# Second layer of a two-layer transformer kernel: fifteen contexts projected before the first batch, and x3 laid into the PSUM bank by ScalarE

## The chip, the cores and the metric

One Trainium2 chip, one of its cores. The kernel is one program for the core's five engines: TensorE (PE in the profile, its weight loads PEld), VectorE (DVE), ScalarE (ACT), GpSimd (POOL) and SyncE (SP, which here issues most DMAs). The metric is device time in microseconds, the median of several executions. One further execution is profiled; its rows give start and duration of each instruction.

## The reference

The input is 16 batches of 256 rows by 256 columns, with a context of 120 rows per batch. There are two layers. The first is attention and a mixture of experts; it fills the first 820 us and the change does not touch it. The second layer, cut to what matters:

```python
x = x + attention(layernorm(x), ctx, ctx, mask, Wq, Wk, Wv)   # gives x4 from x3
x = x + linear(quantise(layernorm(x)), quantise(weight)) + bias
# attention: K = ctx Wk, V = ctx Wv, softmax(Q K^T / 16, masked) V, one head of 256
# quantise: blocks of 32, scale = max|x| / 7.5, nearest point of the FP6 grid, times the scale
```

Everything is float32 on TensorE. The kernel multiplies Wk and Wq together beforehand, so that a batch's scores need only the normalised rows and one projected context ("keys"), and the values are a second projection of the same context.

## The kernel before

`second_phase` is written as one program per engine. A batch goes through some twenty steps on four engines, and the batches are overlapped by hand: a loop over a cycle number c runs on each engine (`CYCLES`, from -4 to 19), and in one cycle the engine does step A of batch c, step B of batch c-1, step C of batch c-3 and so on. Each engine works through its list strictly in order and waits on semaphores, so the order of the calls in each loop sets what can hide behind what.

The names that matter, with n the batch:

- Contexts. `turn_context(n)` (PE transposes, L2313), `keep_context` (ACT, L2181), `keys(n)` (PE, L2336), `keep_keys` (ACT, L2185), `values(n)` (PE, L2344), `keep_values` (ACT, L2189). The first `EARLY` = 9 contexts are projected in a loop ahead of the cycles, while the rows of the first batches are still being fetched and normalised. The other seven are projected inside cycles -1 to 5, one in each.
- Rows. `stats_acc`, `centre`, `residual` (DVE) build x3 from the experts' sum and the residual x2; `stats_x3` (DVE), `inverse_std(N3)` (POOL), `normalise_x3` (ACT, L2154), `turn_rows` (PE, L2325), `keep_xnT` (ACT, L2175).
- Attention. `scores` (PE, L2357) into the bank `zp_ps`, `bounded` (DVE, L2098 and L2102), `exps` (ACT, L2199), `inverse_sums` (DVE, L2125), `diagonals` (ACT, L2211), `turn_probs` (PE, L2367), `keep_probsT` (ACT, L2220), `weigh` (PE, L2377). `weigh` adds to a PSUM bank `f_ps` (a ring of three, one per batch) that already holds x3: `start_result` (PE, L2287) put it there with a matmul of the identity. So after `weigh` the bank holds x4.
- Second norm, quantisation and the last matmul. `stats_x4` (DVE, L2040, reading f_ps), `inverse_std(N4)` (POOL, L1993 to L2002), `normalise_x4` (ACT, L2154, reading f_ps), `scales` (DVE), `to_blocks` (POOL, L2011), `round_blocks` (ACT, L2228), `scale_back` (POOL, L2020), `turn_quantised` (PE, L2278), `keep_xdT` (ACT, L2236), `linear` (PE, L2298 for the bias and L2303), `keep_result` (ACT, L2243), and the store by SP.

The expert phase's last matmul ends on PE before the contexts begin; the rows of the experts' sum are loaded only when the last scattered additions of the expert phase have landed (`past["added"]` in SP's list).

Of the kernel before, what the change touches and what calls it, by code (L numbers as in the profile page):

```python
# [56 lines left out]
RING = 3  # L57
# [1736 lines left out]
def second_phase(nc, sem, past, ident, second, mask, x2_d, acc_d, ctx, out):  # L1794
# [7 lines left out]
    with st:  # L1802
# [101 lines left out]
        s_dg = sem("c_diagonal_ready")  # L1904
        s_xn4 = sem("c_xn4_ready")
# [28 lines left out]
        EARLY = 9  # L1934
# [4 lines left out]
        def sync(sp):  # L1939
# [35 lines left out]
            for c in range(-5, B + 4):  # L1975
                if exists(c - 2):
                    sp.wait_ge(s_o, c - 1)
                    sp.dma_start(rows(out, c - 2), o[c % 2][:]).then_inc(s_ost[c % 2], 16)
                if RING <= c + 5 < B:
                    load_x2(c + 5)  # L1980
                if RING <= c + 8 < B:
                    load_acc(c + 8)
# [3 lines left out]
        def gpsimd(pool):  # L1986
# [40 lines left out]
            for c in CYCLES:  # L2027
                inverse_std(NA, c + 3, s_x3)
                inverse_std(N3, c + 2, s_xn3)
                to_blocks(c - 1)  # L2030
                inverse_std(N4, c, s_xn4)
                scale_back(c - 1)

        def vector(dve):
# [104 lines left out]
            for c in CYCLES:  # L2139
                bounded(c)  # L2140
                residual(c + 2)
                inverse_sums(c)
                stats_x3(c + 2)
                centre(c + 3)
                scales(c - 1)
                stats_acc(c + 4)
                stats_x4(c)

        def scalar(act):
# [64 lines left out]

            def keep_probsT(n):
                if not exists(n):
                    return
                act.wait_ge(s_pT_p, n + 1)
                ge(act, s_o_p, n - 1)
                act.copy(pT[n % 2][0:CTX], pT_ps).then_inc(s_pT, 1)  # L2220
# [30 lines left out]
            for c in CYCLES:  # L2251
                exps(c - 1)
                normalise_x4(c - 2)
                diagonals(c - 1)
                if late(c + 9):
                    keep_keys(c + 9)
                keep_result(c - 4)
                keep_probsT(c - 1)
                if late(c + 9):
                    keep_values(c + 9)  # L2260
                keep_xdT(c - 3)
                keep_xnT(c)
                if EARLY < c + 10 < B:
                    keep_context(c + 10)
                normalise_x3(c + 1)
                round_blocks(c - 2)

        def tensor(pe):
# [12 lines left out]

            def start_result(n):
                if not exists(n):
                    return
                pe.wait_ge(s_x3, n + 1)
                ge(pe, s_o, n - 2)
                pe.matmul(f_ps[n % RING][:].rearrange("p u d -> p (u d)"), ident[:],  # L2287
                          x3[n % RING][:].rearrange("p u d -> p (u d)"),
                          start=True, stop=False, skip_group_check=True)
# [81 lines left out]
            def weigh(n):  # L2371
# [3 lines left out]
                pe.wait_ge(s_v, n + 1)  # L2375
                for u in range(2):
                    j = pe.matmul(f_ps[n % RING][:, u, :], pT[n % 2][0:CTX, u, :], vv[n][0:CTX, :],  # L2377
                                  start=False, stop=True, skip_group_check=True)
# [7 lines left out]
            for s, value in past["experts"]:  # L2386
                pe.wait_ge(s, value)
            for c in CYCLES:
                turn_quantised(c - 3)
                turn_probs(c - 1)  # L2390
                start_result(c - 1)
                weigh(c - 1)
                if EARLY < c + 10 < B:
                    turn_context(c + 10)
# [3 lines left out]
                if late(c + 10):  # L2398
                    keys(c + 10)
                if late(c + 10):  # L2400
                    values(c + 10)
# [25 lines left out]
```

## Time and profile before

| | us |
|---|---|
| median of 3 runs | 972.43 |
| lowest, highest | 972.27, 979.09 |
| the profiled execution | 978.93 |
| span of its instructions | 977.2 |
| last expert matmul group ends on PE, first context turned | 819.55 |
| context 1 turned (starts) | 820.46 |
| last early `values` starts (ninth context) | 837.31 |
| first `scores` (batch 0) | 843.31 |
| `scores`, eight matmuls: after a wait, and in a stream | 1.12, 1.05 |
| `linear`, eight matmuls in the steady cycle | 1.99 |
| `weigh` of batches 0, 2, 15 | 848.60, 862.46, 959.27 |

Times inside the profile are counted from the start of the span. PE is busy 97% of the span, yet in a pipelined kernel this is an average: whether PE or a chain of waits sets the pace has to be read stage by stage. A start of one instruction less the start of the next on the same engine is the distance that counts for a queue, since consecutive instructions overlap a little; an instruction that waits for another one's result starts only after the recorded end of that other one.

### The profile page before, as it was taken

How to read it: one execution, taken by the hardware profiler on the slowest of the kernel's cores; microseconds unless marked ns; L12 is line 12 of the kernel's file. 1: busy time of each engine (PE TensorE's matmuls, PEld its weight loads, DVE VectorE, ACT ScalarE, POOL GpSimd, SP SyncE). 2: the span in 40 equal slices, each digit the busy share in tenths (PEclk: the TensorE clock that was granted, in tenths of full speed). 3: DMA queues.
4: the chain of work that ended last, by engine and by line, in shares of the span. 5: the costliest groups of instructions: out<-in, count | busy, mean ns of one | idle time of the engine just before them, and what ended most of it. 6: DMA issues, size and time to landing. Idle time of an engine off the chain costs nothing.

```text
span 977.2 us, 22166 instructions
## 1 busy us (share of the span) xinstructions
PE 944.5 (97%) x7195; PEld 804.6 (82%) x7195; DVE 515.9 (53%) x1268; ACT 519.7 (53%) x1326; POOL 495.2 (51%) x660
## 2 busy tenths in 40 slices
PE   6999999999989999998999999999999999899997
PEld 4777777677758999998999999999999998777774
DVE  3788898888874543533223223232232232787862
ACT  3777877777754743333333333333333333678884
POOL 2444344565763148765554444445344442576773
PEclk9999999999999999999999999999999999999999
DMA  5234454355433455333342221222222217423311
GB/s 171 88 121 151 139 173 133 101 151 160 147 115 99 143 161 70 33 34 47 48 65 39 42 40 29 39 34 35 43 33 39 39 32 188 122 86 93 115 53 46
DMA packets 86126, 85.38 MB, mean 87 GB/s; under 512 B 19296, under 2 KB 81184, under 8 KB 85888
## 3 DMA queue, kind: packets, MB, share of 16 engines
q1 hardware_dynamic: 70336, 65.28, 21.9%
q0 software_dynamic: 15680, 18.69, 13.1%
q8 instruction: 62, 1.02, 0.5%
q14 instruction: 48, 0.39, 0.2%
HBM read 52.54 MB, written 31.39 MB: 86 GB/s over the span
## 4 chain that ended last, share of the span: by engine, by line
PE 88%; DVE 3%; issue 2%; ACT 2%; POOL 2%; another core or an unknown queue 1%; SPq 1%; DMA 1%; DVEq 0%; POOLq 0%; ACTq 0%
PE b_H L1582 25%; PE b_Y L1603 24%; PE a_T L939 5%; PE a_O L953 4%; PE c_f_ps L2303 3%; PE a_S L919 3%; PE a_M L988 3%; PE a_O L894 2%; PE c_f_ps L2298 2%; PE b_xT L1571 2%; PE a_T L905 2%; PE c_f_ps L2287 1%; PE c_zp_ps L2357 1%; PE c_f_ps L2377 1%
## 5 line engine op out<-in xcount | busy, mean ns | idle before, releaser
L1752 ACT ACTIVATE b_hiddenT<-b_H,b_b 128x128 f32<-128x128 f32 x568 | 162.3, 369 | 320.5 <-PE b_H L1582 276.9
L1582 PEld LDWEIGHTS b_H<-b_rowsT,b_w 128*128 128x128 f32 x2272 | 264.7, 192 | 7.4 <-ACT b_rowsT L1759 3.0
L1582 PE MATMUL b_H<-b_rowsT,b_w 128*128 128x128 f32 x2272 | 265.6, 275 | 2.8 <-ACT b_rowsT L1759 2.6
L1603 PE MATMUL b_Y<-w_sb,b_hiddenT 128*128 x1136 | 257.5, 379 | 1.1 <-issue 1.0
L1521 POOL DMA_INDIRECT ffn_rows<-b_y,b_slots x71 | 138.7, 1953 | 197.3 <-DVE b_y L1687 115.3
L1603 PEld LDWEIGHTS b_Y<-w_sb,b_hiddenT 128*128 128x128 f32 x1136 | 210.4, 190 | 27.7 <-issue 2.0
L1683 DVE TENSOR_TENSOR b_y<-b_Y,b_b 128x256 f32<-128x256 f32 x71 | 30.2, 425 | 300.2 <-PE b_Y L1603 279.2
L1510 POOL DMA_INDIRECT b_rows<-xn_rows,b_slots x71 | 75.3, 1060 | 68.0 <-PE b_xT L1571 49.7
L1670 DVE COPY b_w<-w_sb 128x2048 f32 x71 | 87.8, 1237 | 35.3 <-issue 29.8
L1243 ACT COPY a_probsT<-a_T 120x512 f32<-120x512 f32 x128 | 74.8, 586 | 46.2 <-PE a_T L939 37.3
L423 POOL DMA_INDIRECT buckets<-r_pay,r_place x64 | 70.6, 1103 | 24.4 <-issue 19.4
L1076 DVE TENSOR_REDUCE a_max<-a_S 128x8 f32<-128x960 f32 x64 | 73.6, 1150 | 13.4 <-PE a_S L919 13.1
L939 PE MATMUL a_T<-ident,a_probs 128*120 128x128 f32 x512 | 77.0, 278 | 3.3 <-ACT a_probs L1235 3.1
L1084 DVE TENSOR_TENSOR a_probs<-a_S,a_max 128x960 f32<-128x960 f32 x64 | 73.2, 1144 | 0.7
L939 PEld LDWEIGHTS a_T<-ident,a_probs 128*120 128x120 f32 x512 | 56.8, 138 | 15.7 <-issue 9.3
L1235 ACT ACTIVATE a_probs<-a_probs 128x960 f32<-128x960 f32 x64 | 64.5, 1008 | 9.0 <-DVE a_probs L1084 6.8
L953 PE MATMUL a_O<-a_probsT,a_vaug 120*32 120x128 f32 x1024 | 54.3, 285 | 0.4 <-ACT a_probsT L1243 0.3
L953 PEld LDWEIGHTS a_O<-a_probsT,a_vaug 120*32 120x32 f32 x1024 | 20.2, 108 | 28.9 <-issue 23.1
L785 POOL TENSOR_TENSOR a_x<-a_x,a_xin 128x256 f32<-128x256 f32 x16 | 12.4, 774 | 48.2 <-DVE a_x L1097 43.0
L988 PE MATMUL a_M<-a_wsg,a_xn2T 128*128 128x264 f32 x128 | 35.6, 401 | 0.2 <-ACT a_xn2T L1258 0.2
L919 PE MATMUL a_S<-a_kbd,a_qT 32*128 32x240 f32 x512 | 35.0, 387 | 0.9 <-ACT a_qT L1219 0.8
L2303 PEld LDWEIGHTS c_f_ps<-c_wdT,c_xdT 128*128 128x128 f32 x128 | 23.4, 193 | 14.8 <-issue 12.1
(237 smaller groups left out, 1322.5 us busy)
## 6 DMA issues: line engine op xcount, KB each, us to landing
w_sb<-in_L_ffn_W SPq DMA_DIRECT2D x32, 512.0 KB
x_rows<-a_x SPq DMA_DIRECT2D x32, 128.0 KB
xn_rows<-a_xn SPq DMA_DIRECT2D x32, 128.0 KB
shared_rows<-a_shared SPq DMA_DIRECT2D x32, 128.0 KB
b_spare<-shared_rows SPq DMA_DIRECT2D x16, 256.0 KB
ffn_rows<-b_spare SPq DMA_DIRECT2D x16, 256.0 KB
c_x<-x_rows SPq DMA_DIRECT2D x16, 256.0 KB, 3.0
c_acc<-ffn_rows SPq DMA_DIRECT2D x16, 256.0 KB, 2.7
```

Of the source, the lines that this page charges most:

```text
L423: pool.indirect_dma_start(bucket_d, IndirectOffsetOnAxis(place[:, t, k:k + 1], 0), pay[:, t, k, :], None).then_inc(s_put[g // 2], 16)
L939: i = pe.transpose(T_ps[q % 2][0:CTX, j * P:(j + 1) * P], pr[q // 2][:, 4 * (q % 2) + j, :], ident[:])
L953: i = pe.matmul(O_ps[VB * j:VB * (j + 1), q * P:(q + 1) * P], vaug[t // 2 % 2][0:CTX, 4 * q + j, :], pT[q % 2][0:CTX, j, :], start=True, s ...
L1076: dve.tensor_reduce(mx[h][:].rearrange("p (r j) -> p r j", r=RG), scores_of(h), AX.X, ALU.max).then_inc(s_mx, 1)
L1084: dve.tensor_tensor(pr[h][:].rearrange("p (r j) c -> p r j c", r=RG), scores_of(h), mx[h][:].rearrange("p (r j) -> p r j", r=RG).unsqueeze ...
L1243: act.copy(pT[q % 2][0:CTX].rearrange("p j n -> p (j n)"), T_ps[q % 2][0:CTX, :]).then_inc(s_T, 1)
L1510: pool.indirect_dma_start(xg[n % AHEAD][:], None, xn2_d, IndirectOffsetOnAxis(iw[:].bitcast(I32)[:, n, 0:1], 0)).then_inc(s_x[n % AHEAD], 16)
L1521: pool.indirect_dma_start(acc_d, IndirectOffsetOnAxis(iw[:].bitcast(I32)[:, n, 0:1], 0), y[n % KEPT_Y][:], None, bounds_check=TOK + SPARE - 1,
L1582: j = pe.matmul(H_ps[i][:, c * P:(c + 1) * P], w1c[i][:, k * HID + c * P:k * HID + (c + 1) * P], xT[:, k * P:(k + 1) * P], start=(k == 0), ...
L1603: j = pe.matmul(y_ps[i][:, 0:D], hT[i][:, c * P:(c + 1) * P], w2_sb[:, bass.ds(e * (HB * D) + c * D, D)], start=(c == 0), stop=(c == HB - 1))
L1670: dve.tensor_copy(w1c[i][:], w1_sb[:, bass.ds(e * (KC * HID), KC * HID)])
L1752: j = act.activation(hT[i][:, c * P:(c + 1) * P], H_ps[i][:, c * P:(c + 1) * P], ACT.Gelu, bias=b1c[i][:, c:c + 1])
```

## The change

Three things are done, and the loops are put in another order.

1. `EARLY` is 15: fifteen contexts are projected ahead of the cycles, and only the sixteenth inside cycles -1 and 0. The loads, turns and keeps move with them; none is added or dropped.
2. `start_result` on PE is gone. A new step `lay_x3(n)` on ACT copies x3 into the bank f_ps, between `keep_result` and `keep_probsT`. It waits for the semaphore of `keep_result`, the instruction just ahead of it in ACT's own queue. `weigh` waits for it. So that a matmul that adds finds the bank in the state it needs, each of the three banks gets one matmul of 128x512 ahead of the cycles (discarded values).
3. Orders. On PE, `turn_probs` and `turn_quantised` trade places and move to the end of a cycle's list (with their batch numbers one up, so in time only the two are exchanged). On DVE the list is only rotated: the sequence in time is the same. On POOL, `scale_back` moves from ahead of the next `inverse_std(NA)` to behind it. On ACT, `keep_xnT` and `keep_context` go ahead of `keep_xdT`. SP issues the loads of x2 one cycle earlier and those of the experts' sum one cycle later, relative to the stores.

```diff
--- before.py
+++ after.py
@@ -1902,6 +1902,8 @@
         s_o_p = sem("c_x4_psum")
         s_rs = sem("c_rs_ready")
         s_dg = sem("c_diagonal_ready")
+        s_laid = sem("c_x3_laid")
+        s_banks = sem("c_banks_written")
         s_xn4 = sem("c_xn4_ready")
         s_am = sem("c_amax_ready")
         s_sc = sem("c_scale_ready")
@@ -1931,7 +1933,7 @@
 
 
 
-        EARLY = 9
+        EARLY = 15
 
         def late(n):
             return EARLY <= n < B
@@ -1972,14 +1974,14 @@
                 load_acc(n)
             for n in range(CTX_RING + 2, B):
                 load_context(n)
-            for c in range(-5, B + 4):
+            for c in range(-4, B + 4):
                 if exists(c - 2):
                     sp.wait_ge(s_o, c - 1)
                     sp.dma_start(rows(out, c - 2), o[c % 2][:]).then_inc(s_ost[c % 2], 16)
-                if RING <= c + 5 < B:
-                    load_x2(c + 5)
-                if RING <= c + 8 < B:
-                    load_acc(c + 8)
+                if RING <= c + 6 < B:
+                    load_x2(c + 6)
+                if RING <= c + 7 < B:
+                    load_acc(c + 7)
             for i in range(2):
                 sp.wait_ge(s_ost[i], 8 * B)
 
@@ -2026,10 +2028,10 @@
             pool.memset(ones[:], 1.0).then_inc(s_tie, 1)
             for c in CYCLES:
                 inverse_std(NA, c + 3, s_x3)
+                scale_back(c - 2)
                 inverse_std(N3, c + 2, s_xn3)
                 to_blocks(c - 1)
                 inverse_std(N4, c, s_xn4)
-                scale_back(c - 1)
 
         def vector(dve):
             def stats(g, src, n):
@@ -2137,14 +2139,14 @@
                 bounds(part)
             dve.wait_ge(second["s_vec"], 32)
             for c in CYCLES:
+                residual(c + 1)
+                inverse_sums(c - 1)
+                stats_x3(c + 1)
+                centre(c + 2)
+                scales(c - 2)
+                stats_acc(c + 3)
+                stats_x4(c - 1)
                 bounded(c)
-                residual(c + 2)
-                inverse_sums(c)
-                stats_x3(c + 2)
-                centre(c + 3)
-                scales(c - 1)
-                stats_acc(c + 4)
-                stats_x4(c)
 
         def scalar(act):
             def normalise(g, dst, src, n, done):
@@ -2211,6 +2213,15 @@
                     j = act.activation(dg[n % 2][:, u, :], ident[:], ACT.Identity,
                                        scale=rs[n % 2][:, u:u + 1])
                 j.then_inc(s_dg, 1)
+
+            def lay_x3(n):
+                if not exists(n):
+                    return
+                act.wait_ge(s_x3, n + 1)
+                if n == 0:
+                    act.wait_ge(s_banks, RING)
+                ge(act, s_o, n - RING + 1)
+                act.copy(f_ps[n % RING][:], x3[n % RING][:]).then_inc(s_laid, 1)
 
             def keep_probsT(n):
                 if not exists(n):
@@ -2252,16 +2263,17 @@
                 exps(c - 1)
                 normalise_x4(c - 2)
                 diagonals(c - 1)
-                if late(c + 9):
-                    keep_keys(c + 9)
+                if late(c + 15):
+                    keep_keys(c + 15)
                 keep_result(c - 4)
+                lay_x3(c - 1)
                 keep_probsT(c - 1)
-                if late(c + 9):
-                    keep_values(c + 9)
+                if late(c + 15):
+                    keep_values(c + 15)
+                keep_xnT(c)
+                if EARLY < c + 16 < B:
+                    keep_context(c + 16)
                 keep_xdT(c - 3)
-                keep_xnT(c)
-                if EARLY < c + 10 < B:
-                    keep_context(c + 10)
                 normalise_x3(c + 1)
                 round_blocks(c - 2)
 
@@ -2278,15 +2290,6 @@
                         j = pe.transpose(xdT_ps[:, u, k, :],
                                          xd[n % 2][:, u, k * P:(k + 1) * P], ident[:])
                 j.then_inc(s_xdT_p, 1)
-
-            def start_result(n):
-                if not exists(n):
-                    return
-                pe.wait_ge(s_x3, n + 1)
-                ge(pe, s_o, n - 2)
-                pe.matmul(f_ps[n % RING][:].rearrange("p u d -> p (u d)"), ident[:],
-                          x3[n % RING][:].rearrange("p u d -> p (u d)"),
-                          start=True, stop=False, skip_group_check=True)
 
             def linear(n):
                 if not exists(n):
@@ -2373,6 +2376,7 @@
                     return
                 pe.wait_ge(s_pT, n + 1)
                 pe.wait_ge(s_v, n + 1)
+                pe.wait_ge(s_laid, n + 1)
                 for u in range(2):
                     j = pe.matmul(f_ps[n % RING][:, u, :], pT[n % 2][0:CTX, u, :], vv[n][0:CTX, :],
                                   start=False, stop=True, skip_group_check=True)
@@ -2385,20 +2389,24 @@
                 values(n)
             for s, value in past["experts"]:
                 pe.wait_ge(s, value)
+
+            for bank in f_ps:
+                pe.matmul(bank[:].rearrange("p u d -> p (u d)"), ident[:],
+                          wdT[:].rearrange("p k d -> p (k d)"), start=True, stop=True,
+                          skip_group_check=True).then_inc(s_banks, 1)
             for c in CYCLES:
-                turn_quantised(c - 3)
-                turn_probs(c - 1)
-                start_result(c - 1)
                 weigh(c - 1)
-                if EARLY < c + 10 < B:
-                    turn_context(c + 10)
+                if EARLY < c + 16 < B:
+                    turn_context(c + 16)
                 scores(c)
                 linear(c - 3)
                 turn_rows(c + 1)
-                if late(c + 10):
-                    keys(c + 10)
-                if late(c + 10):
-                    values(c + 10)
+                if late(c + 16):
+                    keys(c + 16)
+                if late(c + 16):
+                    values(c + 16)
+                turn_probs(c)
+                turn_quantised(c - 2)
 
         return Programs(sync, gpsimd, tensor, vector, scalar)
 
```

## Rows read from the trace of the kernel before

**Rows 1.** The page: busy time of each engine over the whole span.

```profile
PE 944.5 (97%) x7195; PEld 804.6 (82%) x7195; DVE 515.9 (53%) x1268; ACT 519.7 (53%) x1326; POOL 495.2 (51%) x660
```

**Rows 2.** Busy time by stretch, mostly weigh to weigh: stretch, length, busy by engine, granted clock.

```profile
838.35:843.31 4.96, 2.59 (x19) 2.25 (x19) 3.03 (x11) 2.73 (x8) 3.30 (x8) 1.00 0.45 132
848.60:855.53 6.93, 5.93 (x38) 4.63 (x36) 5.94 (x22) 5.18 (x16) 4.33 (x12) 1.00 0.25 77
871.39:880.31 8.92, 8.92 (x52) 6.96 (x50) 6.41 (x23) 6.80 (x19) 5.87 (x12) 1.00 0.30 89
910.37:917.36 6.99, 6.99 (x38) 5.25 (x37) 6.30 (x24) 5.90 (x17) 5.63 (x13) 1.00 0.39 115
968.00:977.20 9.20, 5.24 (x18) 3.15 (x16) 0.00 (x0) 1.76 (x3) 0.47 (x1) 0.85 0.16 57
```

**Rows 3.** Timeline of PE: first and last early values, then the first batch.

```profile
821.59 1.03 PE L2344 MATMUL c_v_ps<-c_wv,c_ctxT 128*120 128x256 f32 x4
...
837.31 1.03 PE L2344 MATMUL c_v_ps<-c_wv,c_ctxT 128*120 128x256 f32 x4
839.89 0.63 PE L2325 MATMUL c_xnT_ps<-ident,c_xn 128*128 128x128 f32 x4 [1.54 <-ACT c_xn L2154]
...
843.31 1.12 PE L2357 MATMUL c_zp_ps<-c_gT,c_xnT 128*128 128x120 f32 x8 [0.83 <-ACT c_xnT L2175]
```

**Rows 4.** SP's queue: the last six context loads are issued.

```profile
830.13 2.88 SPq L1946 DMA_DIRECT2D c_ctx<-in_ctx  x6
```

**Rows 5.** The chain that ended last, one steady cycle: start, length, what.

```profile
908.71 0.44 PE c_xdT_ps L2278 x4
909.15 0.44 PE c_zp_ps L2367 x4
909.59 0.95 PE c_f_ps L2287 x2
```

**Rows 6.** Timeline of DVE in a steady cycle.

```profile
911.44 0.76 DVE L2040 BATCH_NORM_STATS2 c_x_bn<-c_f_ps 128x6 f32<-128x256 f32 x2 [0.33 <-PE c_f_ps L2377]
912.40 0.38 DVE L2098 SCALAR_TENSOR_TENSOR c_z<-c_zp_ps,c_bound 128x240 f32<-128x240 f32 x1
```

**Rows 7.** Timeline of POOL, the same cycle.

```profile
913.91 0.20 POOL L2002 TENSOR_TENSOR c_x_nb<-c_x_nm,c_x_rstd 128x2 f32<-128x2 f32 x1
914.06 1.05 POOL L2020 TENSOR_TENSOR c_xd<-c_q,c_amax 128x512 f32<-128x512 fp8e4 x1
915.08 0.23 POOL L1993 TENSOR_SCALAR c_acc_ve<-c_acc_mv 128x2 f32<-128x2 f32 x1
...
916.29 0.22 POOL L1993 TENSOR_SCALAR c_x_ve<-c_x_mv 128x2 f32<-128x2 f32 x1
```

**Rows 8.** Timeline of ACT, the same cycle.

```profile
913.25 0.40 ACT L2199 ACTIVATE c_probs<-c_z,c_nmax 128x120 f32<-128x120 f32 x1 [0.68 <-DVE c_nmax L2102]
...
914.21 1.02 ACT L2154 ACTIVATE c_xn<-c_f_ps,c_x_nb,c_x_rstd 128x256 f32<-128x256 f32 x2
915.12 0.69 ACT L2211 ACTIVATE c_diagonal<-ident,c_rs 128x128 f32<-128x128 f32 x2
915.71 0.57 ACT L2243 COPY c_out<-c_f_ps 128x512 f32<-128x512 f32 x1
```

**Rows 9.** Timeline of ACT in batch 0, and PE's weight load behind it.

```profile
846.45 0.70 ACT L2211 ACTIVATE c_diagonal<-ident,c_rs 128x128 f32<-128x128 f32 x2 [0.23 <-DVE c_rs L2125]
...
847.94 0.37 ACT L2220 COPY c_probsT<-c_zp_ps 120x256 f32<-120x256 f32 x1 [0.55 <-PE c_zp_ps L2367]
...
852.48 1.02 ACT L2154 ACTIVATE c_xn<-c_f_ps,c_x_nb,c_x_rstd 128x256 f32<-128x256 f32 x2
...
848.36 0.43 PEld L2377 LDWEIGHTS c_f_ps<-c_v,c_probsT 120*128 120x128 f32 x2 [0.43 <-ACT c_probsT L2220]
```

**Rows 10.** Groups of ACT by shape, whole span: busy, mean ns of one.

```profile
L1461 ACT ACTIVATE b_spare<-b_spare 128x512 f32<-128x512 f32 x16 | 9.6, 651 | 0.0
L2243 ACT COPY c_out<-c_f_ps 128x512 f32<-128x512 f32 x16 | 9.3, 580 | 5.2 <-PE c_f_ps L2303 5.2
```

**Rows 11.** Timeline of PE: the linear layer of batch 14, in the drain.

```profile
966.44 2.90 PE L2303 MATMUL c_f_ps<-c_wdT,c_xdT 128*128 128x256 f32 x8
```

## The prediction

> **What bounds the kernel now.** The page [rows 1] shows PE busy 97% of the span. That invites the reading that taking work off PE is worth its length, so the second layer has to be read in parts. The windows [rows 2] are cut from one `weigh` (W below) to the next. Three regimes are seen. From 848.60 to 855.53 PE is busy 5.93 of 6.93 us: although a context is projected in that cycle, PE waits for others. From 871.39 to 880.31 it is busy all 8.92 us, again with a context. From 910.37 to 917.36, with no context, it is busy all 6.99 us, while DVE has 6.30 and ACT 5.90. So contexts cost nothing in the first two cycles and about 1.93 us in each of the next three (W2 to W5, with numbers for batches).
>
> How near is the next limit in the steady cycle? Follow one batch's x4 through the timelines. W starts at 910.37; DVE's `stats_x4` starts at 911.44 [rows 6]; POOL ends the N4 factors at 913.91 + 0.20 = 914.11 [rows 7]; ACT's `normalise_x4` starts at 914.21 [rows 8]. That is 3.84 us. ACT's next instruction is `diagonals` for the batch behind (0.91 later, 915.12), and `turn_probs` and `weigh` of that batch need it. This closes a loop with a length of one cycle: W, stats_x4, N4, normalise_x4, diagonals, turn_probs, W. Before the change it closes over PE: diagonals to turn_probs is 0.70 of duration and 0.04 to start, then 0.44 and 0.95 for turn_probs and start_result [rows 5, 9]: 3.84 + 0.91 + 0.74 + 0.44 + 0.95 = 6.88. PE's own list takes 6.99. Only 0.11 us separate PE, which looks like the bound, from this chain. That distance is what the case turns on.
>
> **The change, part by part.**
>
> *Six more contexts in front.* The early loop repeats every (837.31 - 821.59) / 8 = 1.965 us [rows 3]. Six more: +11.79. ACT's `normalise_x3` of batch 0 stands behind all `keep_values` in ACT's list, so it moves too; nothing of the first batch gets on PE earlier. Their loads were all issued by 830.13 + 2.88 = 833.01 [rows 4]. The first of them (context 10) is turned at about 820.46 + 9 x 1.965 = 838.2, 5 us later: no stall.
>
> *Three bank matmuls.* Each is a 128x512 matmul like start_result, 0.86 in its shorter form (0.95 in rows 5): 2.6 us. Before `turn_rows` of batch 0, PE now waits 1.54 [rows 3], which hides that much. Left: +1.04. With 0.95 each it would be +1.3.
>
> *First batches.* `scores` of batch 0 follows 3.42 after its turn_rows [rows 3], as before, since one context (now the sixteenth) still stands between. Scores to diagonals takes 3.14 (843.31 to 846.45). From diagonals to `keep_probsT` is 1.49 [rows 9], set by turn_probs; `lay_x3` fits in front of it (0.59 + about 0.52 = 1.11). From keep_probsT to W I take 0.50: 0.37 of duration and 0.13, between the weight load's 0.42 (848.36 - 847.94) and 0.60. So scores to W is 5.13 instead of 5.29 (-0.16). The next two periods were 6.93 each. Now they are W to normalise_x4 3.88 (848.60 to 852.48) + 0.91 + 1.49 + 0.50 = 6.78: -0.15 each, -0.30.
>
> *Steady cycle, W2 to W15, 13 periods.* From batch 3 on `keep_result` stands in ACT's list as well. The loop now runs diagonals, keep_result, lay_x3, keep_probsT, all in one queue. W to normalise_x4 3.84, to diagonals 0.91, to keep_result 0.59 [rows 8]. lay_x3 waits for keep_result's own semaphore: it starts after its recorded end, 0.57 + 0.04 = 0.61, instead of overlapping it by 0.10 as ACT's instructions otherwise do (914.21 + 1.02 against 915.12), which would be 0.47. Lay_x3 itself: no row has ACT writing PSUM. The nearest ones [rows 10] are a PSUM to SBUF copy of this shape, 0.580, and an SBUF to SBUF activate, 0.651; less about 0.10 of overlap that gives 0.48 to 0.55; I take 0.52. keep_probsT to W 0.50. W now starts on an idle PE, for which I add 0.06 (the eight matmuls of `scores` took 1.12 after a wait and 1.05 in a stream). Sum: 3.84 + 0.91 + 0.59 + 0.61 + 0.52 + 0.50 + 0.06 = 7.03 us. PE's list is down to 6.99 - 0.95 = 6.04 and no longer matters. Thirteen periods took 959.27 - 862.46 = 96.81 and now take 91.4: -5.4. All of that comes from the context cycles that got shorter, and none from start_result.
>
> The Trainium skill ("ScalarE: Activation LUTs", section "Step-by-step: what each stage is for") says that an ACTIVATE into PSUM is faster than one into SBUF. By that the lower end, 0.48, would hold, 0.5 us less in all. The same page's "Rules for kernel authors" gives about 0.3 us and 0.83 ns per element, an estimate of 0.72 for 512 elements, some 1.8 us more in all. Neither is used in the sum.
>
> *Orders.* Moving `scale_back` behind inverse_std(NA) puts it 916.29 - 915.08 = 1.21 us later [rows 7], ending (15.27 + 1.05 against 14.21) about 2.10 after normalise_x4 starts; turn_quantised, 0.60 or so, then runs until 2.75, ahead of W at 3.13. The cover is 0.38; without it the excess would come on each period. The rotated DVE list changes nothing in time. keep_xnT ahead of keep_xdT follows PE's need. SP's loads land well over a cycle ahead in both forms. The last `weigh` to the end of the span (17.93 us, 959.27 to 977.2) keeps its sequence: 0.
>
> *Sum.* +11.79 + 1.04 - 0.16 - 0.30 - 5.4 = +7.0 us on a span of 977.2. The profiled execution took 978.93, 6.5 above the median of 972.43; the runs themselves lie between 972.27 and 979.09. The change is local, so I put the same difference on the median: 979.4 us.
>
> **Rivals.**
>
> - *The ACT stretch hides, DVE sets the pace.* If keep_result and lay_x3 cost 0.76 instead of 1.13, DVE's own list is next: 6.99 less its idle 0.33 [rows 6] = 6.66. Then 13 x 6.66 = 86.6, and the total is +2.2: 974.6. For it: the terms are small. Against it: the wait on keep_result is in the code. A result below the old time needs a period under about 6.5, under DVE's list; 2 in 100.
> - *Slower, by the same loop at its upper ends.* The price is the period: the self-wait at 0.75 instead of 0.61, lay_x3 at 0.61, keep_probsT to W 0.60, W on an idle PE 0.07 more. That is 7.03 + 0.14 + 0.09 + 0.10 + 0.01 = 7.37 and 13 x 0.34 = +4.4: 983.8. It decides against the kernel by over 1% from a period of 7.24 on.
> - *TensorE's clock.* PE will idle about 1.0 us per cycle in two pieces. In the drain the clock is 0.85 [rows 2], and `linear` of batch 14 took 2.90 [rows 11] where it takes 1.99 at the full level (of 1.2 and 2.4 GHz). If that came in each cycle, turn_probs would be reached 0.57 late and more; a period of about 7.5, 13 x 0.47 = +6.1: 985.5. Against it: from 838.35 on PE is busy 2.59 of 4.96, then 5.93 of 6.93, and the clock stays 1.00 [rows 2]. The Trainium skill ("TensorE: Matmul & The Clock Gate", section "What's actually happening") has the rule behind it: the default is throttled and activity releases it, so idle that a change adds to PE can cost more than its length.
> - *PE is the bound as the page says* and the period falls to 6.04: 13 x 6.04 = 78.5, a total of -5.9, 966.5. The 0.11 us of slack and DVE's list speak against it; it is the kernel's hoped-for case, and I count it in the 2 in 100 above.
>
> **How the numbers follow.** Forecast (period 6.85 to 7.2) 0.65, DVE sets the pace 0.14, upper ends 0.12, clock 0.05, below the old time 0.02, something unseen 0.02. The likeliest gives 979.4. For the range: below, the DVE case at 974.6 is nearly taken in; above, the upper ends at 983.8, and room for a median that falls at the upper of the times shown: 975.0 to 985.5. About 1% (9.7 us) is what a measurement of this kernel can tell from no change: the bounds are 962.7 and 982.2. Faster 0.02. Slower: upper ends, clock, and a median from the upper of the times shown (0.06), 0.23. The same: 0.75.
>
> **What would show it.** Early `values` would run fifteen times, to about 849; the first scores would start near 856.1, W0 near 861.2, W2 near 874.8, W15 near 966. In the steady cycle PE would idle about 1.0 us before turn_probs and before W, with ACT named as the releaser, lay_x3 would start 0.04 after keep_result ends, and the period would be 7.03 with the clock at 1.00. The prediction is wrong if the period is 6.7 or less, if PE is still busy without a gap, or if W to normalise_x4 is no longer 3.8.

## The result

The changed kernel takes 985.7 us (median of 4, 983.68 to 989.32) where the kernel before takes 972.35 (median of 4, 971.3 to 979.09). The ratio is 1.014, with a 95% interval of 1.011 to 1.017: slower by 13.4 us. I had forecast 979.4 and a range up to 985.5. The direction is right (the chance I gave to "slower by over 1%" was 0.23), the size is half of what came, and the result lies just outside the range.

The page of the profile answers to [rows 1]: PE is busy a little less, and the kernel is longer.

```profile
PE 942.2 (95%) x7169; PEld 805.3 (82%) x7169; DVE 522.6 (53%) x1268; ACT 530.3 (54%) x1342; POOL 497.8 (50%) x660
```

The span is 987.6 us. What lies ahead of the second layer is the same program in both kernels (817.17 us here, 819.55 before, and between 811 and 821 in the runs below), so the profiles are compared from the first context turned to the end of the span. Each column is cut from the timeline of PE by the same instructions (us):

| part | before | forecast | changed kernel |
|---|---|---|---|
| first context turned to first `turn_rows` | 20.34 | 33.2 | 33.01 |
| to `weigh` of batch 0 (W0) | 8.71 | 8.55 | 8.95 |
| W0 to W2 | 13.86 | 13.56 | 16.61 |
| W2 to W15 | 96.81 | 91.4 | 94.84 |
| W15 to the end | 17.93 | 17.9 | 17.02 |
| sum | 157.65 | 164.6 | 170.43 |

The sum grows by 12.78, in line with the medians' 13.35. The forecast's 7.0 is short by 5.8: 3.05 in the first two periods, 3.4 in the thirteen after them, 0.4 ahead of W0; the drain gave 0.9 back and the front 0.2.

The windows from weigh to weigh answer to [rows 2] (stretch, length, busy time of PE, PEld, DVE, ACT, POOL, granted clock):

```profile
859.13:867.38 8.25, 5.32 (x21) 4.35 (x21) 5.41 (x19) 4.73 (x14) 3.99 (x11) 0.69 0.19 64
867.38:875.74 8.36, 5.66 (x24) 5.12 (x25) 6.80 (x25) 5.59 (x15) 6.16 (x13) 0.72 0.24 65
875.74:883.66 7.92, 7.54 (x35) 5.58 (x34) 6.78 (x22) 6.31 (x17) 5.47 (x12) 0.86 0.12 38
927.54:934.85 7.31, 6.57 (x35) 4.87 (x35) 6.95 (x24) 6.48 (x17) 5.72 (x13) 1.00 0.34 108
949.46:956.50 7.04, 6.56 (x34) 4.86 (x34) 5.37 (x21) 6.49 (x17) 5.50 (x13) 1.00 0.10 38
```

Two things stand out. In the first three periods TensorE's clock is down, and they are the ones that I had wrong most (by 1.5, 1.6 and 0.9 us). And there are two steady periods, 7.31 from batch 3 to batch 12 and 7.04 behind it: the second is my 7.03.

PE in the first batches (its timeline; the bracket is the idle time before and what ended it):

```profile
857.46 1.21 PE L2370 MATMUL c_zp_ps<-c_diagonal,c_probs 128*120 128x128 f32 x4 [2.33 <-ACT c_diagonal L2213]
859.13 2.07 PE L2381 MATMUL c_f_ps<-c_v,c_probsT 120*128 120x256 f32 x4 [0.46 <-ACT c_probsT L2231]
861.00 1.90 PE L2360 MATMUL c_zp_ps<-c_gT,c_xnT 128*128 128x120 f32 x8
```

`weigh` takes 2.07 us and `scores` 1.90, where they took 1.03 and 1.05 in the steady cycle: the lower of the two levels, 1.2 GHz. Before them PE stands idle for 2.33 us, where a context used to be projected. The lower level comes and goes: by turn_probs of batch 1 the clock was back (0.70 us, at 866.22), and `weigh` behind it was slow again (1.79).

In the steady cycle the timelines of DVE and POOL answer to [rows 6, 7]:

```profile
925.40 1.60 DVE L2055 SCALAR_TENSOR_TENSOR c_centred<-c_acc,c_acc_mv,c_gamma 128x256 f32<-128x256 f32 x2
...
929.01 0.73 DVE L2042 BATCH_NORM_STATS2 c_x_bn<-c_f_ps 128x6 f32<-128x256 f32 x2
```

```profile
924.60 0.71 POOL L2000 TENSOR_TENSOR c_acc_rstd<-c_acc_ve,c_minus_half 128x2 f32<-128x2 f32 x1
925.28 1.05 POOL L2022 TENSOR_TENSOR c_xd<-c_q,c_amax 128x512 f32<-128x512 fp8e4 x1
```

The pair of `centre` takes 1.60 us; before it took 0.85 in every cycle. It starts 0.12 us after `scale_back`, which runs to 926.33. The instructions of this line over the whole span, before and now (shortest, median, longest in ns):

```profile
L2053 DVE SCALAR_TENSOR_TENSOR c_centred<-c_acc,c_acc_mv,c_gamma x32: 450/476/486, 832.6 to 936.5; 128x256 f32<-128x256 f32 x32
L2055 DVE SCALAR_TENSOR_TENSOR c_centred<-c_acc,c_acc_mv,c_gamma x32: 450/476/1207, 830.1 to 948.5; 128x256 f32<-128x256 f32 x32
```

`stats_x4` at 929.01 has no idle time in front of it: DVE has become the bound, and W (927.54) to stats_x4 is 1.47 instead of 1.07.

ACT's timeline answers to [rows 8]:

```profile
924.43 1.02 ACT L2156 ACTIVATE c_xn<-c_f_ps,c_x_nb,c_x_rstd 128x256 f32<-128x256 f32 x2
925.34 0.68 ACT L2213 ACTIVATE c_diagonal<-ident,c_rs 128x128 f32<-128x128 f32 x2
925.93 0.58 ACT L2254 COPY c_out<-c_f_ps 128x512 f32<-128x512 f32 x1
926.59 0.59 ACT L2224 COPY c_f_ps<-c_x 128x512 f32<-128x512 f32 x1
927.12 0.37 ACT L2231 COPY c_probsT<-c_zp_ps 120x256 f32<-120x256 f32 x1
```

keep_result to lay_x3 is 0.66 (forecast 0.61), lay_x3 to keep_probsT 0.53 (0.52), keep_probsT to weigh 0.42 (0.50 and 0.06 for the idle PE), diagonals to keep_result 0.59.

### The profile page after: what moved, and what is told of

Read it like the earlier page. It is cut to its first block, busy times and chain, and to the rows that moved or that the text cites. A ratio compares the mean times of both kernels' runs of the same rounds, so it can differ in the third digit from the quotient of the medians.

```text
span 987.6 us, 22137 instructions
## 1 busy us (share of the span) xinstructions
PE 942.2 (95%) x7169; PEld 805.3 (82%) x7169; DVE 522.6 (53%) x1268; ACT 530.3 (54%) x1342; POOL 497.8 (50%) x660
## 4 chain that ended last, share of the span: by engine, by line
PE 82%; DVE 9%; ACT 3%; issue 3%; POOL 2%; DMA 2%; POOLq 0%; SPq 0%; DVEq 0%; ACTq 0%
PE b_H L1582 26%; PE b_Y L1603 25%; PE a_T L939 5%; PE a_O L953 4%; PE a_M L988 3%; PE a_O L894 3%; PE a_S L919 3%; PE a_T L905 2%; DVE c_x_bn L2042 2%; PE b_xT L1571 2%; PE c_v_ps L2347 1%; DVE c_centred L2055 1%; PE c_xdT_ps L2339 1%; PE a_O L880 1%; PE a_M L965 1%
## 5 line engine op out<-in xcount | busy, mean ns | idle before, releaser
L423 POOL DMA_INDIRECT buckets<-r_pay,r_place x64 | 71.0, 1110 | 24.1 <-issue 18.4
```

The costliest lines, as they stand in the source:

```text
L423: pool.indirect_dma_start(bucket_d, IndirectOffsetOnAxis(place[:, t, k:k + 1], 0), pay[:, t, k, :], None).then_inc(s_put[g // 2], 16)
```

## The experiments

Two causes are to be tested, each against a rival: the clock in the first batches (theory 2) and the collision of `centre` with `scale_back` (theory 1). The times of the runs scatter by several us from chip to chip and run to run, so beside the ratio each run is read by the parts of its one profiled execution, which repeat to some hundredths where the clock is at 1.00. Each ratio is to the kernel before, run beside it on the same chip.

### GpSimd's order put back

```diff
             for c in CYCLES:
+                scale_back(c - 2)
                 inverse_std(NA, c + 3, s_x3)
-                scale_back(c - 2)
                 inverse_std(N3, c + 2, s_xn3)
```

> The changed kernel with scale_back put back ahead of inverse_std(NA) on GpSimd. Theory 1 (VectorE's centre is held up while GpSimd's scale_back runs): every pair of centre takes about 0.85 us again instead of 1.60, the period from weigh to weigh of batches 3 to 12 falls from 7.31 us to the 7.04 us that the changed kernel has once no centre is left, and the time falls by about 9 x 0.27 = 2.4 us. Rival (ScalarE's queue with the added copy sets 7.31): the period stays at 7.31 and the time does not move. The first two periods (8.25 and 8.36 us) stay in either case.

Measured: every period from batch 4 on is 7.03 or 7.04, and centre is back:

```profile
926.68 0.85 DVE L2055 SCALAR_TENSOR_TENSOR c_centred<-c_acc,c_acc_mv,c_gamma 128x256 f32<-128x256 f32 x2
```

W3 to W15 falls from 86.92 to 84.81 us, 2.1 (expected 2.4). The ratio to the kernel before is 1.0126 (1.0101 to 1.0151), which can't be told from that of the change (1.011 to 1.017): the gain is seen in the periods, not in the medians. The profile's first three periods were 8.16, 8.96 and 8.38 with the clock down, so part of the gain was lost there. The sum is 168.81. Theory 1 holds; ScalarE's queue does not make 7.31.

### GpSimd's order alone, in the kernel before

```diff
             for c in CYCLES:
                 inverse_std(NA, c + 3, s_x3)
+                scale_back(c - 2)
                 inverse_std(N3, c + 2, s_xn3)
                 to_blocks(c - 1)
                 inverse_std(N4, c, s_xn4)
-                scale_back(c - 1)
```

> The kernel before with only scale_back moved behind the next inverse_std(NA) on GpSimd, as the change does. Theory 1: centre takes 1.60 us in the steady cycle, VectorE's list becomes 6.66 + 0.75 and the period of batches 5 to 12 rises from 6.99 to about 7.3 to 7.4 us: +2.3 to +3 us. Rival (the order on GpSimd is free, since it is busy 5.6 of 7 us): no change.

Measured: a ratio of 1.0062 (1.0042 to 1.0083) and a sum of 162.96, +5.3. The steady period is 7.57 to 7.58, more than either account gave.

```profile
918.33 1.60 DVE L2053 SCALAR_TENSOR_TENSOR c_centred<-c_acc,c_acc_mv,c_gamma 128x256 f32<-128x256 f32 x2
```

```profile
919.32 0.65 PE L2278 MATMUL c_xdT_ps<-ident,c_xd 128*128 128x128 f32 x4 [0.46 <-POOL c_xd L2020]
```

The collision comes as expected, but it is not what sets 7.57. `stats_x4` starts 1.07 us after W (913.53 and 914.60), as before, 0.15 us behind the instruction ahead of it, so VectorE is not yet the bound. What sets the period is that PE waits 0.46 us for the late result of scale_back, since in this kernel turn_quantised stands ahead of turn_probs; the changed kernel exchanges these two, and there turn_quantised has no wait in front of it. So this run shows that the order alone makes centre 1.60 us long; the price of the collision in the changed kernel is that of the first experiment, and the +5.3 here is not it (0.4 of it is the drain).

### Work for TensorE in the first batches

```diff
                 turn_rows(c + 1)
+                if c in range(0, 3):
+                    pe.wait_ge(s_v, B)
+                    for _ in range(3 - (c == 0)):
+                        pe.matmul(v_bank[:], ident[:], wdT[:].rearrange("p k d -> p (k d)"),
+                                  start=True, stop=True, skip_group_check=True)
```

> The changed kernel with 2, 3 and 3 unused matmuls of 128x512 into the free bank of the values in cycles 0, 1 and 2 (8 matmuls, about 6.9 us of TensorE work that it would otherwise idle). Theory 2 (the first batches are slow because TensorE, idle without the contexts, falls to 1.2 GHz): the granted clock stays at 1.00, weigh of batch 0 to weigh of batch 2 takes 13.6 instead of 16.6 us, batch 2 to 3 about 7.3 instead of 7.9, and the time falls by about 3.5 us although work was added. Rival (the first batches are slow by their chain over VectorE, GpSimd and ScalarE alone): no change, or slower by what the added matmuls delay.

Measured: the mean clock over the span is 1.000, W0 to W2 takes 13.26 (two periods of 6.63) instead of 16.61, W2 to W3 7.67 instead of 7.92 (7.3 expected; it is 7.03 once GpSimd's order is put back as well, below), and the sum is 166.29: 4.1 us less with 8 matmuls more. The ratio of the times is 1.0121 (1.0089 to 1.0153); its interval overlaps that of the change, so the gain is shown by the parts and not by the medians. The two windows that hold W0 to W2:

```profile
859.90:866.50 6.60, 5.92 (x27) 3.65 (x27) 5.80 (x22) 4.85 (x14) 4.24 (x12) 1.00 0.25 82
866.50:873.10 6.60, 6.15 (x30) 4.03 (x30) 6.31 (x22) 5.46 (x15) 5.08 (x12) 1.00 0.24 79
```

Work that nobody needs makes the stretch 3.35 us shorter. By the rival, a chain over the other engines alone, it would have stayed. With the clock up that chain is the 6.63 (forecast 6.78).

### Fifteen early contexts alone, in the kernel before

```diff
-        EARLY = 9
+        EARLY = 15
```

(with the loops' offsets 9 and 10 made 15 and 16)

> The kernel before with 15 early contexts instead of 9 and nothing else. My account (a context in front costs 1.965 us each, one in a cycle costs 1.93 only in cycles 3 to 5 and nothing in 0 to 2): +11.8 in front, -5.9 in the three cycles of 8.92 us, so +5.9 us; if the clock falls in the first batches, some 3 us more, +9. Rival (contexts cost the same wherever they stand, since TensorE is busy 97%): 0.

Measured: a ratio of 1.0074 (1.0044 to 1.0104), a sum of 166.54, +8.9 us. Front +11.8, W0 to W2 +2.8 with the clock down, W2 to W15 -6.1 (90.70), drain +0.4. A context in front costs its length; in the first cycles it costs nothing and keeps the clock up; only the three later cycles give TensorE's time for it back. W0 to W1 took 9.60 and W1 to W2 7.09; a window that holds most of W0 to W1:

```profile
860.00:870.00 10.00, 7.11 (x24) 5.27 (x23) 7.39 (x28) 5.50 (x16) 5.90 (x14) 0.70 0.26 79
```

### Both causes mended

> The changed kernel with both edits of the first two runs: scale_back ahead of inverse_std(NA), and 2, 3 and 3 unused matmuls in cycles 0 to 2. If the two causes are the whole error of my forecast and are independent, the clock stays at 1.00, weigh of batch 0 to 2 takes 13.3 us, the thirteen periods after it 7.04 each (91.5 us), and from the first context turned to the end of the span it takes 33.0 + 8.4 + 13.3 + 91.5 + 17.0 = 163.2 us against 157.65 before: slower by 5.6 us, near the +7.0 that I had forecast. If something else is at work it is 165 or more.

(The edit is that of the first and the third experiment together.) Measured: 33.01 + 8.44 + 13.25 + 91.37 = 146.07 up to W15, where 146.2 was expected. All thirteen periods are 7.02 or 7.03. The drain took 18.41 instead of 17.0, so the sum is 164.48. The ratio is 1.0065 (1.0041 to 1.0089), 6.4 us on 978 (the medians, 983.08 and 978.12, differ by 5.0). On another chip the first edit alone had 1.0126 and the filler alone 1.0121, with intervals that begin at 1.0101 and 1.0089, so the two together show in the times as well. Up to W15 the changed kernel takes 153.41, with the filler 149.29, with both 146.07, and my forecast was 146.7: taken in this order the clock is worth 4.1 us and GpSimd's order 3.2. The two causes are thus the error of the forecast up to W15, and the sum with both mended is +6.8, where I had worked out +7.0.

### Half of the copy

```diff
-                act.copy(f_ps[n % RING][:], x3[n % RING][:]).then_inc(s_laid, 1)
+                act.copy(f_ps[n % RING][:, 0, :], x3[n % RING][:, 0, :]).then_inc(s_laid, 1)
```

> The first of those edits alone (GpSimd order put back), and lay_x3 copies only the first of the two halves of x3, 256 instead of 512 columns (left out: the second half, so the second half of the rows is not right). Theory (the steady period of 7.04 us is the loop weigh, stats_x4, N4, normalise_x4, diagonals, keep_result, lay_x3, keep_probsT, which has no slack): the copy is shorter by about 0.2 us and the period falls by the same, to about 6.84. Rival (VectorE's or TensorE's list sets 7.04): it stays at 7.04.

(On top of GpSimd's order put back; one execution.) Measured: 6.82 or 6.83 in each steady period, where the first experiment had 7.04. The copy is 0.38 instead of 0.59 us, and the next instruction follows 0.31 after it instead of 0.52.

```profile
932.08 0.38 ACT L2224 COPY c_f_ps<-c_x 128x256 f32<-128x256 f32 x1
932.39 0.37 ACT L2231 COPY c_probsT<-c_zp_ps 120x256 f32<-120x256 f32 x1
```

A copy shorter by 0.21 us shortens every steady period by 0.21 to 0.22. With the collision away, the loop through ScalarE sets the steady cycle, without slack.

### Nine early contexts, the rest of the change kept

```diff
-        EARLY = 15
+        EARLY = 9
```

> The changed kernel with nine early contexts, as before: the copy on ScalarE, the bank matmuls and the orders alone. My account: front 20.3 + 1.0 us for the bank matmuls, no loss of clock in the first batches (a context stands in each cycle), TensorE's 7.97 instead of 8.92 us in the three cycles with context and full list (3 x -0.95), then 7.31 instead of 6.99 while centre collides with scale_back (about 7 x +0.32) and 7.04 after (3 x +0.05): about +0.5 us from the first context to the end, against +12.8 for the whole change. Rival (the copy on ScalarE is what makes the change slow): +5 us or more.

Measured: a ratio of 1.0028 (1.0000 to 1.0057) and a sum of 159.05, +1.4 us. W0 to W2 is 13.59, steady 7.30 and then 7.03, as expected; but the three context cycles took 8.62, 8.55 and 8.56, not 7.97. My account left out what start_result had covered: without it PE waits between turn_quantised and weigh for keep_probsT (0.17 us). The timeline of ACT says more: in such a cycle keep_keys waits 0.62 us for `keys`, and keep_result, lay_x3 and keep_probsT follow it in the same queue, 1.88 us from keep_keys (888.24) to W (890.12). That this queue sets 8.55 is read from the timeline and not tested by itself. Of the 12.8 us of the change, all but 1.4 come with the six contexts in front.

### Nine early contexts, order put back, short bank matmuls

```diff
+            half_ident = ident[:].bitcast(BF16)
             for bank in f_ps:
-                pe.matmul(bank[:].rearrange("p u d -> p (u d)"), ident[:],
-                          wdT[:].rearrange("p k d -> p (k d)"), start=True, stop=True,
-                          skip_group_check=True).then_inc(s_banks, 1)
+                for u in range(2):
+                    j = pe.matmul(bank[:, u, :], half_ident[:, 0:P], half_ident,
+                                  start=(u == 0), stop=(u == 1), skip_group_check=True)
+                j.then_inc(s_banks, 1)
```

> Nine early contexts, the copy on ScalarE, GpSimd's order put back, and the three bank matmuls made in bfloat16 (two of 128x256 each, some 0.3 us a bank instead of 0.9), so that they fit into the 1.54 us that TensorE waits there anyway. Account: front 20.3, first batches 8.5 + 13.6, batches 2 to 15 three periods of 7.97 and ten of 7.04 = 94.3, tail 17 to 18: about 154.3 us against 157.65 before, 3 us faster than the kernel before. Rival (the copy is of no use anywhere): no faster than before.

Measured: front 20.25, so the bank matmuls are hidden; steady 7.03; context cycles 8.55 again; sum 156.74, 0.9 less than before. The ratio is 1.0015 (0.9988 to 1.0042): no difference that can be told. The 3 us that I expected did not come: 1.7 of them lie in batches 2 to 15, most of that in the context cycles, and the rest in the drain (18.39).

### turn_probs ahead of the context

```diff
+                if c >= 3:
+                    turn_probs(c)
                 if late(c + 10):
                     keys(c + 10)
                 if late(c + 10):
                     values(c + 10)
-                turn_probs(c)
+                if c < 3:
+                    turn_probs(c)
```

(on top of the previous kernel, with keep_keys behind keep_probsT on ScalarE from cycle 4 on)

> The previous kernel (nine early contexts, copy on ScalarE, GpSimd's old order, short bank matmuls) with turn_probs ahead of keys and values on TensorE from cycle 3 on, and keep_keys behind keep_probsT on ScalarE from cycle 4 on. In the three cycles with a context and a full list TensorE idled 0.34 us behind turn_probs, since start_result no longer covers keep_probsT, and the wait was seen as a period of 8.55. With the context matmuls between turn_probs and weigh the period should be TensorE's own list, 8.0: 3 x -0.5 = -1.5 us, 155.2 from the first context to the end (before: 157.65). Rival (the 8.55 is TensorE's own work): no change.

Measured: a miss. The context cycles took 8.85, 8.75 and 8.75, the ratio is 1.0001 (0.9974 to 1.0029).

```profile
873.12 0.70 PE L2372 MATMUL c_zp_ps<-c_diagonal,c_probs 128*120 128x128 f32 x4 [0.38 <-ACT c_diagonal L2213]
```

turn_probs now comes before its diagonals are ready, and the context matmuls stand between it and weigh: the loop got longer by the very work that had lain beside it.

### A fourth bank, the copy out of the loop

```diff
+        FOUR = 7
+        f_ps = [f_ring[n % RING] if n < FOUR else (v_full, f_ring[1], f_ring[2], f_ring[0])[(n - FOUR) % 4]
+                for n in range(B)]
...
-                lay_x3(c - 1)
+                if c - 1 < FOUR:
+                    lay_x3(c - 1)
...
                 round_blocks(c - 2)
+                if c >= FOUR:
+                    lay_x3(c)
```

(The diff is cut to its main lines. It stands on top of the previous kernel; e11 is the same with turn_probs and keep_keys back where the changed kernel has them.)

> As e9, and from batch 7 on the bank of the values, free by then, is a fourth bank in the ring, so that lay_x3 no longer needs keep_result just before it and stands at the end of ScalarE's cycle, outside the loop. The loop is then weigh to normalise_x4 3.84, diagonals 0.91, 1.49 over turn_probs to keep_probsT, 0.43 to weigh = 6.67, beside VectorE's list of 6.6: a period of 6.65 to 6.75 instead of 7.03 for the eight periods from batch 7 on, -2.5 us, about 152.5 from the first context to the end, 5 us less than before. Rival (keep_result and lay_x3 are not what sets 7.03): no change against e9.

> As e10 with the fourth bank, but with turn_probs and keep_keys where they stand in the changed kernel (e9's edit made the three context cycles 8.75 to 8.85 instead of 8.55 to 8.62, since turn_probs then waits 0.38 us for the diagonals and the context matmuls stand between it and weigh). Account: 20.3 + 8.5 + 13.6 + 3 cycles of 8.57 + 7.0 + 9 of 6.74 + 17 to 18 = 152.6 from the first context to the end, against 157.65 before and 153.2 in e10: 0.5 us faster than e10, about 0.5 per cent faster than the kernel before. Rival (the gain of e10 was the spread of the runs): a ratio of 1.00.

Measured: with the fourth bank the steady period is 6.73 to 6.75 from batch 6 on in both. The first of the two (with the misplaced turn_probs) has a ratio of 0.9961 (0.9926 to 0.9996) and a sum of 153.17. The second has 0.9931 (0.9908 to 0.9954), 968.11 against 974.41 us in the same group of runs: it beats the kernel before by 0.7% (0.5% expected), and the changed kernel, which took 985.16 us in that group, by 17 us. Its profiled execution has a sum of 157.71 all the same, since in it the clock was at the lower level through the drain, which took 21.95 instead of 17.0. Up to W15 it took 135.76, against 139.72 before. The window in the drain:

```profile
957.00:969.20 12.20, 8.26 (x18) 4.64 (x17) 0.00 (x0) 1.75 (x3) 0.00 (x0) 0.50 0.12 43
```

The copy now stands behind round_blocks, and the queue between diagonals and keep_probsT waits for turn_probs instead (ACT's timeline, e10):

```profile
939.64 0.58 ACT L2230 COPY c_f_ps<-c_x 128x512 f32<-128x512 f32 x1
...
942.63 0.57 ACT L2260 COPY c_out<-c_f_ps 128x512 f32<-128x512 f32 x1
943.51 0.37 ACT L2237 COPY c_probsT<-c_zp_ps 120x256 f32<-120x256 f32 x1 [0.31 <-PE c_zp_ps L2381]
```

### The change once more

> The changed kernel itself once more, beside the others on one chip. The parts should repeat: 33.0 from the first context turned to the first turn_rows, 9.0 to weigh of batch 0, 16.6 to 17 to batch 2 with the clock below 0.9, 7.31 in the steady cycles with centre, 7.04 after; a ratio of 1.011 to 1.017 to the kernel before.

Measured: 33.01, 8.82, 17.65 (more than the 16.6 to 17 expected: 8.76 and 8.89, with the clock at 0.50 and 0.69 in them), 7.30 and 7.03; a ratio of 1.0114 (1.0085 to 1.0143). The lower clock in the first batches stands in every profile with fifteen early contexts and no filler, its length not quite the same.

## Why the prediction was right in sign and short in size

*What bounds the kernel.* Right. PE at 97% was not the bound to go by: the loop over stats_x4, N4, normalise_x4 and ScalarE's queue was 0.11 us behind it by my sum, and taking 0.95 us off PE bought nothing in the steady cycle. The steady period without the collision is 7.04, 7.03 forecast, and halving the copy moved it one for one.

*Six contexts and the bank matmuls in front.* Right: 12.67 measured, 12.83 forecast.

*First batches.* This is the step that failed most: -0.30 forecast, +2.75 measured. The chain was worked out well (6.63 with the clock up, 6.78 forecast), but at the lower clock weigh and scores take nearly twice as long (2.07 and 1.90 us), and they then make a longer way round: the softmax of the next batch stands ahead of normalise_x4 in ACT's list, and it waited for those scores.

```profile
863.81 0.40 ACT L2201 ACTIVATE c_probs<-c_z,c_nmax 128x120 f32<-128x120 f32 x1 [3.21 <-DVE c_nmax L2104]
```

W to normalise_x4 took 5.45 in this period (3.88 forecast, 3.82 in the filled run), which is more than the whole of the 1.47 by which the period was off. The clock was among my rivals, at 0.05, and I looked for it in the steady cycle. There it stayed at 1.00 with PE busy 6.57 of 7.31. What I held against it was that the clock stays up in the first batches of the kernel before, with PE busy 2.59 of 4.96 and then 5.93 of 6.93 [rows 2]. Those 5.93 contain the context that the change takes out: I had used a row of before for a stretch whose content the change removes. Less the 1.96 of the context and the start_result, PE's share is near 3.1 of 6.8, and no row of before shows that from one weigh to the next. The row of 2.59 of 4.96 is as thin, but it is one stretch alone, and the one behind it was full in the kernel before. From the first scores to W0, before and in the changed kernel:

```profile
843.31:848.60 5.29, 4.92 (x31) 3.79 (x32) 3.91 (x13) 3.57 (x13) 0.99 (x3) 1.00 0.05 15
853.58:859.13 5.55, 2.76 (x16) 2.22 (x17) 4.15 (x14) 3.30 (x11) 1.26 (x3) 0.85 0.14 47
```

The Trainium skill ("TensorE: Matmul & The Clock Gate", section "What's actually happening") says that activity is what keeps the throttle off; here the filled run (5.92 of 6.60, clock 1.00) and the change (5.32 of 8.25, 0.69, much of it at half speed) agree with it. The 0.4 us ahead of W0 have the same cause: that part is 8.95 where turn_probs of batch 0 took 1.21, and 8.44 in the runs with the filler, where it took 0.70.

*Orders.* The second failure. I priced the later scale_back by its reader alone (0.38 us of cover, which held in the changed kernel) and put its effect on DVE at nothing. (That the rotated list of DVE is free was right: with it and GpSimd's old order the period is 7.04.) In the kernel before, scale_back ran from 914.06 to 915.11 [rows 7], and centre began just clear of it (the timeline of DVE of the kernel before):

```profile
915.18 0.85 DVE L2053 SCALAR_TENSOR_TENSOR c_centred<-c_acc,c_acc_mv,c_gamma 128x256 f32<-128x256 f32 x2
```

Moved by 1.21 us in my sum and by 1.00 as measured against the start of normalise_x4, it lies on centre. The pair grows by 0.75, the 0.33 us of idle that DVE had is gone, and DVE's list, 7.31, is the period. (6.66 and 0.75 would be 7.41; stats_x4 also starts 0.08 us closer to the instruction ahead of it once it need not wait.) W to normalise_x4 becomes 4.21 (920.22 to 924.43), which my own list of signs has as one of being wrong. Nine periods at 0.28 over the forecast are 2.5 us, and W2 to W3, where both causes act, 0.9. The Trainium skill ("SBUF — State Buffer", section "Who interferes with whom") has a rule for it: a VectorE instruction with two inputs in SBUF contends with a GpSimd instruction that reads SBUF, for a shared pair of ports that only one of them can hold. The rows agree: centre has two inputs in SBUF, and its longest instance is 1207 ns against 476, while stats_acc, whose bn_stats have one input, was not longer beside to_blocks (0.68 us the pair at 928.12 in the changed kernel, 0.74 without it at 858.31). No wait shows in the trace; the instruction is only longer.

*The lay_x3 stretch.* Terms right within 0.08: the wait for its own engine costs a start 0.08 after the recorded end (0.04 assumed), and keep_probsT to weigh was 0.08 shorter. From W at 949.46 the period of 7.04 is 3.93 to normalise_x4, 0.92, 0.58, 0.67, 0.52 and 0.42; my terms were 3.90 (with the 0.06 of the idle PE), 0.91, 0.59, 0.61, 0.52 and 0.50. The mechanism is right, but that the sum agrees to 0.01 is luck: errors of up to 0.08 cancel. A copy from SBUF to PSUM takes 0.59 us, inside my 0.58 to 0.65. The 0.72 that I worked out from the Trainium skill ("ScalarE: Activation LUTs", section "Rules for kernel authors") did not fit this instruction: the page gives its 0.3 us for an ACTIVATE with a bias operand of [128,1], which this copy does not have. The 1.8 us that I set beside it was also wrong: with the same 0.10 of overlap it would have been 0.62 against 0.52, 1.3 us in thirteen periods. Whether ScalarE is faster into PSUM than into SBUF is not tested here: the copy into PSUM (0.59) reads SBUF, and that into SBUF (0.58) reads PSUM.

*The drain.* Left at 0, measured -0.9, since its clock was up this time (linear of batch 14 took 1.99 instead of the 2.90 of [rows 11]). In the profiles above the drain goes with its clock: 17.0 at 0.98 or 0.99 (five of them), 17.9 to 18.4 at 0.84 to 0.91, and 22.0 at 0.66. Much of the scatter of the times may come from there; that was not tested by itself. The 0.9 is luck, in that it hid part of the other two errors.

*Range.* The upper end, 985.5, came from the single rivals. The two things that came are of two rivals' kind and came together: the clock, in the first batches and not in each cycle, and DVE setting the pace, at 7.31 and not at the 6.66 of my rival.

## What to carry to other kernels

Taking work off the busiest engine is worth nothing when a loop of waits is a tenth of a microsecond behind it; write out that loop, and look for an instruction (here the copy behind keep_result) that can be put outside it. A row of the old trace stands for the new kernel only if the stretch still contains the same work: the projections taken out of the first batches were also what kept TensorE's clock up. When an instruction of GpSimd is moved, look not only at who needs its result but at which two-input VectorE instruction it will lie on.

## What the runs showed of the hardware

- The granted clock was at 0.50 in the first batch once PE had idled 2.33 us before turn_probs, and was 0.69 and 0.72 on average in the next two periods, in which PE was busy 5.32 of 8.25 and 5.66 of 8.36 us, part of it at half speed. Eight unused matmuls, about 6.9 us of them, kept it at 1.00 and made W0 to W2 3.35 us shorter.
- A two-input VectorE instruction of 0.48 us took 1.21 us when it started just behind a GpSimd instruction of 1.05 us, in two kernels alike (a pair took 1.60 instead of 0.85).
- ScalarE copies 128x512 float32 from SBUF to PSUM in 0.59 us and half of that in 0.38 (the copy of results, PSUM to SBUF, took 0.58); behind an instruction on whose semaphore it waits it starts 0.08 us after the recorded end.
